# Seven products of block sums for eight products of blocks in the second shared network

## The chip, the cores and the metric

The kernel runs on one core of a Trainium2 chip. The metric is the device time in microseconds (us), as the median of several runs. A profiled execution gives the times of single instructions.

## The reference

128 samples `x` (64 x 256 each) go through three two-layer networks with a `relu` between the layers: one of five experts, chosen by the sample's type, and two shared ones. A gate (softmax over three values, made from row 0 of the three outputs) mixes them; then comes one step of a reaction and diffusion equation over the 64 x 256 plane of the sample.

```python
s0 = relu(x @ swi[0]) @ swo[0]          # swi: 2 x 256 x 1024, swo: 2 x 1024 x 256
s1 = relu(x @ swi[1]) @ swo[1]
eo = relu(x @ wi[type]) @ wo[type]
w = softmax(relu(concat(eo[:, 0], s0[:, 0], s1[:, 0]) @ g1) @ g2)
x = x + eo * w0 + s0 * w1 + s1 * w2
x = x + zX * lap_x(x) + zY * lap_y(x) + zR * x * (1 - x)
```

All is float32.

## The kernel before, in words

**Numbers.** A float32 operand is cut into a high part in the PE's fp32r format and a low part (the rest). A product is three matmuls: high x high, high x low, low x high. `XH`/`XL` are the two parts of a tile's columns, `SWH`/`SWL` those of the first weights, `HH`/`HL` those of the hidden values; `SWO` holds both parts of the second weights side by side, so one matmul of 512 columns and one of 256 make a block of a second product.

**Passes and steps.** The work is a list of passes, `PASSES`: two for the gate's rows, 22 expert units, and from `FIRST` on the shared networks. There are 16 tiles of 8 samples (512 columns in 4 blocks of 128), and a tile has two passes: an even one with the first shared network (b = 0) and an odd one with the second (b = 1). The last tile's odd pass is made in two halves of 256 columns (`HALVES`). A pass has 8 steps (`c`), one for each 128 of the 1024 hidden values; `g` counts steps over all passes. Each engine has a loop over `g`, which is the order of its work; nothing is planned at run time.

**PE.** In step `g` it makes the first product of `g` (`first_product`, line 946: for two blocks of 128 input rows, three matmuls each of 512 columns, lines 986 to 988, into one of three banks `hbank`) and then the second product of step `g - 2` (`second_product`, line 1028: four blocks, lines 1055 and 1056, summed over the pass in `acc[0..3]`).

**ACT and DVE.** ACT writes the high part of the hidden values of `g` (`hidden_high`, line 1160; `relu`, line 1166), DVE the low part (`hidden_low`, line 646; operation at line 658), which frees the bank and lets the second product run. At a pass's end, in step 1 of the next, ACT scales `acc` by the gate into `EO` (lines 1168 and 1185), and DVE adds the second half of `acc` (`evacuate`, lines 661 and 676), which frees `acc[j]`.

**Beside this.** In an odd pass DVE makes `residual` (line 689) in step 2, `add_shared` (line 697) for the first network in step 3, and `turn_tile` (line 600: the next tile's blocks, loaded by SP, are transposed into `XZ`) in step 4; ACT copies `XZ` to the high part (`tile_high_whole`, line 1158) and DVE subtracts for the low part (`tile_low_whole`, line 605) in step 5. In an even pass DVE makes `add_shared` for the second network of the tile before in step 1 and the equation in steps 2 to 6 (lines 703, 709, 713, 720, 726), with ACT's `quadratic` in step 2; SP moves halo rows of `Y` in between. The order of the parts in DVE's loop body matters here: in a step, `hidden_low(g)` comes before `evacuate`, and both before the block that begins `if FIRST <= n < NP - 1`.

**The end.** The last tile's results are made block by block, in the order 0, 2, 1, 3: `shared_sum` (line 737), `rows_last`, `react_last` (751), `add_x_last` (757), `add_row` (777), `result_last` (line 781; operation 786). POOL makes the sums of neighbours in `SS` (lines 1353 and 1354), SP stores blocks 1, 2 and 3 (line 1487).

Of the kernel before, what the change touches and what calls it, by code (L numbers as in the profile page):

```python
# [5 lines left out]
F32 = mybir.dt.float32  # L6
F32R = mybir.dt.float32r
I32 = mybir.dt.int32
ALU = mybir.AluOpType
# [75 lines left out]


def tile_of(n):
    kind, i = PASSES[n]
    return 0 if kind == PRE else 1 + i if kind == EXP else 1 + NU + i // 2
# [58 lines left out]
for _g, (_n, _c) in enumerate(CHUNKS):  # L148
    RING += [key for key in tile_parts(_n, _c) if key[0] > 1 and key[1] == 1] + [_g]
PLACE = {key: i for i, key in enumerate(RING)}  # L150


def next_tile(n, c):


    if c != (6 if n == FIRST - 1 else 4) or n < FIRST - 1 or n >= NP - 3:
# [85 lines left out]
def cond_resid_program(nc, x, itok, zx, zy, zr, wi, wo, swi, swo, g1, g2, out):  # L242
    eo_d = nc.dram_tensor("eo_scratch", (NS + NSLOT, S, D), F32, kind="Internal").ap()
    ctx = ExitStack()
    with ctx:
# [14 lines left out]
        XH = [sb(f"xh{i}", [128, 1024], F32R) for i in range(2)]  # L260
        XL = [sb(f"xl{i}", [128, 1024], F32R) for i in range(2)]
        RX = sb("rx", [128, 1024])
        XS = [sb(f"xs{i}", [128, 4, D]) for i in range(2)]
# [30 lines left out]
        with ExitStack() as early:  # L294
            EWH = [sb(f"ewh{i}", [128, 2, F], F32R, early) for i in range(2)]
            EWL = [sb(f"ewl{i}", [128, 2, F], F32R, early) for i in range(2)]
            EWO = [sb("ewo0", [128, NC, 2 * D], F32R, early)]

            with ExitStack() as first:
                RW0 = [sb(f"rw0{i}", [128, 1024], F32, first) for i in range(4)]  # L300
            EWO.append(sb("ewo1", [128, NC, 2 * D], F32R, early))
            RW = [sb(f"rw{i}", [128, 1024], F32, early) for i in range(4)]

# [9 lines left out]
        wx = sb("wx", [128, 6, NT])  # L313
        mask16 = sb("mask16", [128, NT])

        hbank = [ctx.enter_context(nc.psum_tensor(f"hbank{i}", [128, 512], F32)) for i in range(HRING)]
# [35 lines left out]
        lapy = sem("lapy")  # L352
        last_row = sem("last_row")
        itok_in = sem("itok_in")
        z_in = sem("z_in")
# [11 lines left out]

        XB, XZ = RW[0:2], RW[2]

        def unit_cols(a):  # L370
# [67 lines left out]
        def bank_free(key):  # L438

            i = RING[PLACE[key] - HRING]  # L440
            if isinstance(i, tuple):
                return t_free, T_AT[i]
            return (h_hi, i + 1 - 2 * NC) if upright(i) else low_done(i)
# [31 lines left out]
        def _(e):  # L475
# [117 lines left out]
            def turn_tile(t):  # L593

                if t == 0:
                    e.wait_ge(*cut_done(1 + NU, 2))
                else:
                    e.wait_ge(xt_lo, t)
                e.wait_ge(xb_in[t % 2], 256 * (t // 2 + 1))
                e.transpose(XZ[:], XB[t % 2][:]).then_inc(xz_done, 1)  # L600

            def tile_low_whole(t):
                tile = 1 + NU + t
                e.wait_ge(xt_hi, t + 1)
                e.tensor_tensor(XL[tile % 2][:], XZ[:], XH[tile % 2][:].bitcast(F32), ALU.subtract).then_inc(xt_lo, 1)

            def gate_masks():
# [52 lines left out]

            def evacuate(n):
# [6 lines left out]
                for j in block_order(n):  # L668
# [111 lines left out]

            def result_last(j):
                t = NT - 1
                rows = last_y[:, 3, :] if j == 2 else EO[1][:, j, :]
                e.wait_ge(dve_seq, AT["row", 2] if j == 2 else AT["rows", j])
                e.wait_ge(dve_seq, AT["last", 3] if j == 2 else AT["lapx", j])
                e.scalar_tensor_tensor(OT[t % 2][:, j, :], rows, WB[:, 4, t:t + 1], QQ[:, j, :], ALU.mult,
                                       ALU.add).then_inc(*V.up())
                AT["result", t, j] = V.n

            for g in range(G + LAG):  # L790
# [28 lines left out]
                if (n, c) == (2, 0):  # L819
                    evacuate(1)  # L820
                    cut_low(2, 2)
                if g < G and (n, c) != (1, NC - 1):
                    hidden_low(g)
# [9 lines left out]
                if g >= LAG and is_last(g - LAG) and CHUNKS[g - LAG][0] < NP - 2 and g - LAG != 2 * NC - 1:  # L833
                    evacuate(CHUNKS[g - LAG][0])
# [37 lines left out]
            add_x_last(2)  # L872
            rows_last(3)
            shared_sum(1)
            add_row(0)
# [3 lines left out]
            e.wait_ge(o_out[(NT - 1) % 2], 16 * ((NT - 1) // 2))  # L879
            result_last(1)  # L880
            shared_sum(3)
            result_last(2)
            react_last(3)
            add_x_last(3)
            result_last(3)

        @block.tensor
        def _(e):
# [138 lines left out]

            def second_product(g):
# [6 lines left out]
                e.wait_ge(*low_done(g))  # L1035
                if PASSES[n][0] == PRE:
# [7 lines left out]
                woc = weights(n)[2]  # L1044
                if c % 4 == 0:
                    e.wait_ge(*cut_done(weight_set(n), 2 + c // 4))
                order = list(block_order(n))
                for i, j in enumerate(order):
                    js = slice(i * 128, (i + 1) * 128)
                    if c == 0 and acc_before(n, j):  # L1050
# [3 lines left out]
                    else:  # L1054
                        e.matmul(acc[j][:, 0:2 * D], HH[:, g % NH, js], woc[:, c, :], start=(c == 0), stop=False)  # L1055
                        m = e.matmul(acc[j][:, D:2 * D], HL[:, g % NH, js], woc[:, c, 0:D], start=False, stop=last)  # L1056
                    if last:
# [20 lines left out]
            for g in range(G + LAG):  # L1078
# [33 lines left out]
                if (n, c) == (2, 0):  # L1112
                    second_product(g - 2)
                    second_product(g - 1)
                if g < G and (n, c) != (1, NC - 1):
                    first_product(g)
# [19 lines left out]
        def _(e):  # L1136
# [30 lines left out]

            def evacuate(n):
                kind, i = PASSES[n]
                for j in block_order(n):  # L1170
                    if kind == EXP:
# [60 lines left out]
            for g in range(G + LAG):  # L1232
# [14 lines left out]
                if (n, c) == (2, 0):  # L1247
                    cut_high(2, 2)
                if g < G and PASSES[n][0] != PRE:
                    hidden_high(g)  # L1250
                if 2 * NC <= g - LAG < G - 2 * NC and is_last(g - LAG):
                    evacuate(CHUNKS[g - LAG][0])
# [20 lines left out]
        def _(e):  # L1273
# [72 lines left out]
            e.tensor_tensor(FIRST_ROW[:, 0:128:16], ident[:, 0:128:16], ident[:, 0:128:16], ALU.add).then_inc(mats, 1)  # L1346

            t = NT - 1
            for j in LAST_ORDER:
                y = inner(t)[:, j, :]  # L1350
                e.wait_ge(dve_seq, AT["last", j])
                e.wait_ge(dve_seq, AT["result", t - 1])
                e.tensor_tensor(SS[:, j, 1:D - 1], y[:, 0:D - 2], y[:, 2:D], ALU.add).then_inc(lapx, 1)
                e.tensor_tensor(SS[:, j, 0:D:D - 1], y[:, 1:D:D - 3], y[:, 1:D:D - 3], ALU.add).then_inc(lapx, 1)

        @block.sync
        def _(e):
# [127 lines left out]
            for j in (1, 2, 3):  # L1485
                e.wait_ge(dve_seq, AT["result", t, j])
                e.dma_start(out_rows(out, t)[:, j * D:(j + 1) * D], OT[t % 2][:, j, :]).then_inc(o_out[t % 2], 16)
# [23 lines left out]
```

## Time and profile before

| | us |
|---|---|
| median of 3 runs (1135.97 to 1136.01) | 1135.98 |
| profiled execution | 1135.78 |
| its span, first to last instruction | 1134.3 |
| PE busy | 1128.2 (99%) |
| weight loads busy (PEld, beside PE) | 963.9 (85%) |
| DVE busy | 674.2 (59%) |
| ACT busy | 455.5 (40%) |
| POOL busy | 78.8 (7%) |

The span is what the profile covers; the profiled execution's own time is 1.5 us longer. "Busy" is time in which at least one instruction of the engine is shown running. Matmuls are pipelined: one is shown for longer than the distance to the next one's start, so the pace is read from starts.

### The profile page before, as it was taken

The page shows a single profiled execution, that of the slowest core. Times are in us where ns is not written, and L with a number is a line of the kernel's source. Part 1 is how long each engine was busy: PE and PEld are TensorE (multiplying, and loading weights), DVE is VectorE, ACT ScalarE, POOL GpSimd, SP SyncE. Part 2 cuts the span into 40 slices and gives each one's busy share as a digit, 9 for nine tenths or more (in the row PEclk, how much of TensorE's full clock was granted, in tenths as well). Part 3 has the DMA queues.
Part 4 walks back from the last instruction along what each step waited for, and adds up shares of the span by engine and source line. Part 5 has one row for each costly group of instructions (what it writes and reads, how often), then busy time and mean ns, then how long its engine had stood idle before and what let it go on. Part 6 is the DMA issues. An engine that isn't in the chain of part 4 may idle for free.

```text
span 1134.3 us, 16608 instructions
## 1 busy us (share of the span) xinstructions
PE 1128.2 (99%) x5968; PEld 963.9 (85%) x5968; DVE 674.2 (59%) x1007; ACT 455.5 (40%) x790; POOL 78.8 (7%) x123
## 2 busy tenths in 40 slices
PE   9999999999999999999999999999999999999998
PEld 8888888888888888888888888888888888888888
DVE  5655666666676645556546556555565465565556
ACT  3554655555565522333333323323333333233233
POOL 1211212112121000000000000000000000000001
PEclk9999999999999999999999999999999999999999
DMA  8655656566565413113123022031131230221200
GB/s 269 178 161 178 197 175 209 168 183 182 175 204 167 114 52 87 28 57 85 22 64 84 14 71 64 30 75 28 57 85 21 64 85 14 72 58 36 75 29 24
DMA packets 111251, 111.82 MB, mean 99 GB/s; under 512 B 78441, under 2 KB 87234, under 8 KB 111170
## 3 DMA queue, kind: packets, MB, share of 16 engines
q1 hardware_dynamic: 96738, 59.64, 19.4%
q0 software_dynamic: 13952, 50.60, 14.8%
q8 instruction: 47, 0.77, 0.3%
q10 hardware_dynamic: 480, 0.53, 0.2%
q14 instruction: 34, 0.28, 0.1%
HBM read 89.40 MB, written 17.04 MB: 94 GB/s over the span
## 4 chain that ended last, share of the span: by engine, by line
PE 99%; DVE 0%; issue 0%; POOL 0%; DVEq 0%; POOLq 0%
PE acc L1055 30%; PE hbank L986 16%; PE hbank L987 16%; PE acc L1056 15%; PE hbank L988 15%; PE acc L1024 1%; PE acc L1041 1%; PE acc L892 0%; PE tbank L934 0%; PE hbank L934 0%; PE acc L1025 0%; PE hbank L959 0%; PE hbank L1003 0%; PE hbank L1004 0%; PE hbank L1002 0%; PE hbank L960 0%
## 5 line engine op out<-in xcount | busy, mean ns | idle before, releaser
L658 DVE SCALAR_TENSOR_TENSOR hl<-hbank,hh 128x512 fp32r<-128x512 f32 (+1 forms) x416 | 272.0, 655 | 421.1 <-ACT hh L1166 420.8
L1166 ACT ACTIVATE hh<-hbank 128x512 fp32r<-128x512 f32 (+1 forms) x416 | 235.9, 568 | 564.7 <-PE hbank L988 561.3
L1055 PE MATMUL acc<-swo,hh 128*128 128x512 f32 x992 | 359.4, 396 | 0.0
L1056 PE MATMUL acc<-swo,hl 128*128 128x256 f32 x992 | 278.1, 280 | 0.0
L1055 PEld LDWEIGHTS acc<-swo,hh 128*128 128x128 f32 x992 | 186.4, 188 | 43.6
L986 PE MATMUL hbank<-xh,swh 128*128 128x512 f32 (+1 forms) x528 | 205.5, 389 | 0.0
L987 PE MATMUL hbank<-xl,swh 128*128 128x512 f32 (+1 forms) x528 | 205.1, 389 | 0.0
L988 PE MATMUL hbank<-xh,swl 128*128 128x512 f32 (+1 forms) x528 | 202.2, 383 | 0.0
L1056 PEld LDWEIGHTS acc<-swo,hl 128*128 128x128 f32 x992 | 187.4, 189 | 9.6
L1055 PE MATMUL acc<-ewo,hh 128*128 128x512 f32 x496 | 180.0, 395 | 0.0
L1056 PE MATMUL acc<-ewo,hl 128*128 128x256 f32 x496 | 139.1, 281 | 0.0
L986 PEld LDWEIGHTS hbank<-xh,swh 128*128 128x128 f32 x528 | 99.2, 188 | 23.2
L988 PEld LDWEIGHTS hbank<-xh,swl 128*128 128x128 f32 x528 | 99.6, 189 | 21.6
L1055 PEld LDWEIGHTS acc<-ewo,hh 128*128 128x128 f32 x496 | 93.1, 188 | 21.0
L987 PEld LDWEIGHTS hbank<-xl,swh 128*128 128x128 f32 x528 | 99.3, 188 | 10.1
L986 PE MATMUL hbank<-xh,ewh 128*128 128x512 f32 (+1 forms) x288 | 107.4, 373 | 0.0
L987 PE MATMUL hbank<-xl,ewh 128*128 128x512 f32 (+1 forms) x288 | 104.7, 364 | 0.0
L988 PE MATMUL hbank<-xh,ewl 128*128 128x512 f32 (+1 forms) x288 | 104.4, 363 | 0.0
L1056 PEld LDWEIGHTS acc<-ewo,hl 128*128 128x128 f32 x496 | 93.6, 189 | 4.2
L986 PEld LDWEIGHTS hbank<-xh,ewh 128*128 128x128 f32 x288 | 54.2, 188 | 9.9
L988 PEld LDWEIGHTS hbank<-xh,ewl 128*128 128x128 f32 x288 | 54.1, 188 | 9.5
L987 PEld LDWEIGHTS hbank<-xl,ewh 128*128 128x128 f32 x288 | 54.5, 189 | 4.5
(215 smaller groups left out, 973.5 us busy)
## 6 DMA issues: line engine op xcount, KB each, us to landing
rw<-in_L_cond_wi POOLq DMA_DIRECT2D x44, 512.0 KB, 4.4
rw<-in_L_cond_wo POOLq DMA_DIRECT2D x44, 512.0 KB, 4.8
eo_scratch<-eo SPq DMA_DIRECT2D x128, 64.0 KB, 2.4
xs<-in_x SPq DMA_DIRECT2D x16, 512.0 KB, 4.3
rw<-in_x SPq DMA_DIRECT2D x256, 32.0 KB, 2.3
ei<-eo_scratch SPq DMA_DIRECT2D x16, 512.0 KB, 5.5
xs<-in_x SPq DMA_DIRECT2D x126, 64.0 KB, 3.3
out<-ot SPq DMA_DIRECT2D x15, 512.0 KB, 6.3
```

What stands on the lines that cost most here:

```text
L658: e.scalar_tensor_tensor(h_slot(HL, g), bank[:, 0:w], 0.0, h_slot(HH, g).bitcast(F32), ALU.max, ALU.subtract).then_inc(h_lo, 1)
L986: e.matmul(to, wh[:, k, cs], xh[k], start=(k == 0), stop=False)
L987: e.matmul(to, wh[:, k, cs], xl[k], start=False, stop=False)
L988: i = e.matmul(to, wl[:, k, cs], xh[k], start=False, stop=(k == 1))
L1024: e.matmul(acc[0][:, 0:2 * D], HH[:, g % NH, hs], woc[:, f, :], start=(f == 0), stop=False)
L1041: e.matmul(acc[0][:, 0:D], HF[:, g % NH, :], raw_rows(n, 2 + c // 4)[:, c % 4, :], start=(c == 0), stop=last).then_inc(acc_done if last el ...
L1055: e.matmul(acc[j][:, 0:2 * D], HH[:, g % NH, js], woc[:, c, :], start=(c == 0), stop=False)
L1056: m = e.matmul(acc[j][:, D:2 * D], HL[:, g % NH, js], woc[:, c, 0:D], start=False, stop=last)
L1166: e.activation(h_slot(HU if upright(g) else HH, g), bank_of(g)[:, 0:w], ACT.Relu).then_inc(h_hi, 1)
```

## The change

**The products.** In the odd passes of tiles 1 to 14 (14 passes), the eight block products of a first product over two steps become seven. A step pair takes hidden values `p` and `p + 4` (of 8 groups of 128), two blocks of 128 input rows, and two halves of 256 columns: a 2 x 2 by 2 x 2 block product. It is made in the manner of Strassen and Winograd, from sums of the blocks. The sums of the weights (`SUMH`, `SUML`) are made once, by POOL, ACT and DVE; the sums of a tile's columns (`th`, `tl`) in the even pass ahead: four sums on DVE in step 0 (`column_sums`, in place in `XZ`), the high part on ACT in step 3, the low part on DVE in step 7. Each product is three matmuls of 256 columns.

**The corners.** Four of the products are added in one PSUM bank (corner), which between them must be copied out by ACT, since its running value is part of several results; DVE adds the other two banks (sides) to the copies. Then come `relu` and low part as before, but from three places: the top half of a pair (512 columns, in SBUF), the lower right (256, SBUF) and the lower left (256, PSUM).

**What moves.** The second products of a changed pass are cut in two around product D; the evacuation of the even pass is spread over steps 1 and 2 of the changed one; `add_shared` of the first network goes from step 3 to 7, `turn_tile` stays in step 4 (now behind the step's own work), ACT's copy of the tile goes to the end of step 5, and `tile_low_whole` from 5 to 6. SP gets two more loads (512 KB each) ahead of the loop over tiles.

**The end.** For block 3 of the last tile DVE makes the sum of neighbours and other steps itself (`last_block`), and POOL makes the result of block 2.

The diff, cut to its core:

```diff
+def seven(n):
+    kind, i = PASSES[n]
+    return kind == SH and i % 2 == 1 and i >= 3 and 0 <= n < NP - 2
...
@@ DVE @@
+            def column_sums(t):
+                x = [[half_block(XZ[:], k, h) for h in range(2)] for k in range(2)]
+                e.wait_ge(xt_lo, t + 1)
+                e.tensor_tensor(x[1][1], x[1][1], x[0][1], ALU.subtract).then_inc(*V.up())
+                e.wait_ge(dve_seq, V.n)
...
+            def column_sums_low(t):
+                e.wait_ge(ts_hi, t)
+                e.tensor_tensor(TL, XZ[:], TH.bitcast(F32), ALU.subtract).then_inc(ts_lo, 1)
...
+            def seven_step(g):
+                n, c = CHUNKS[g]
+                if c % 2 == 0:
+                    if c == 2:
+                        evacuate(n - 1, (3,))
+                    top_left_sum(g)
+                    if c >= 2:
+                        right_low(g - 1)
+                        left_low(g - 1)
+                    return
+                if c == 1:
+                    evacuate(n - 1, (0,))
+                top_right_sum(g)
+                if c == 1:
+                    evacuate(n - 1, (1,))
+                low_right_sum(g)
+                top_low(g - 1)
+                if c == 1:
+                    evacuate(n - 1, (2,))
...
-                    if b == 1 and c == 3:
+                    if b == 1 and c == (7 if seven(n) else 3):
                         add_shared(t, 0)
+                    if seven(n) and c == 4:
+                        turn_tile(t + 1)
+                    if seven(n) and c == 6:
+                        tile_low_whole(t + 1)
+                    if n == FIRST + 1 and c == 7:
+                        weight_sums_low()
+                    if b == 0 and seven(n + 1) and c == 0:
+                        column_sums(t)
+                    if b == 0 and seven(n + 1) and c == 7:
+                        column_sums_low(t)
...
+            scaled_rows()
...
-            result_last(1)
+            result_one()
             shared_sum(3)
-            result_last(2)
-            react_last(3)
-            add_x_last(3)
-            result_last(3)
+            last_block()
@@ PE @@
+            def seven_step(g):
...
+                def product(to, hi, lo, cols, start, stop):
+                    to = to.rearrange("p (j n) -> p j n", n=128)
+                    e.matmul(to, hi, cols[0], start=start, stop=False, skip_group_check=True)
+                    e.matmul(to, hi, cols[1], start=False, stop=False, skip_group_check=True)
+                    return e.matmul(to, lo, cols[0], start=False, stop=stop, skip_group_check=True)
...
+                if c % 2 == 0:
+                    prev = AT_CHUNK[n, 0]
+                    if c == 0:
+                        e.wait_ge(*low_done(prev - 3))
+                        e.wait_ge(ts_lo, SEVENS.index(n) + 1)
+                        e.wait_ge(dve_seq, AT["weight sums"])
...
+                    product(corner, wh[:, 0, at], wl[:, 0, at], x[0][0], True, False).then_inc(p_prod, 1)
...
+                    product(side, wh[:, 1, at], wl[:, 1, at], x[1][0], True, True).then_inc(p_prod, 1)
...
+                    of_sum(other, 3, y[0][1], True, False).then_inc(h_prod, 1)
+                    second_product(g - LAG, (0, 1))
+                    e.wait_ge(p_copy, 4 * q + 1)
+                    of_sum(corner, 0, y[0][0], False, False).then_inc(p_prod, 1)
+                    second_product(g - LAG, (2, 3))
+                    return
+                if c == 1:
+                    second_product(g - LAG, (0, 1))
+                e.wait_ge(p_copy, 4 * q + 2)
+                of_sum(other, 1, x[1][1], False, True).then_inc(p_prod, 1)
+                e.wait_ge(p_copy, 4 * q + 3)
+                of_sum(corner, 2, y[1][1], False, False).then_inc(p_prod, 1)
+                second_product(g - LAG, (2, 3) if c == 1 else None)
+                e.wait_ge(p_copy, 4 * q + 4)
+                product(corner, wh[:, 1, low], wl[:, 1, low], y[1][0], False, True).then_inc(h_prod, 1)
@@ ACT @@
+            def seven_step(g):
...
+                if c % 2 == 0:
+                    e.wait_ge(p_prod, 5 * q + 1)
...
+                    e.activation(TOP[q % 2][:, 0:256], corner, ACT.Copy).then_inc(p_copy, 1)
+                    if c == 2:
+                        evacuate(n - 1, (3,))
+                    if c >= 2:
+                        right_high(g - 1)
...
+                    e.activation(P5_ROOM, other, ACT.Copy).then_inc(p_copy, 1)
+                    if c >= 2:
+                        left_high(g - 1)
+                    e.wait_ge(p_prod, 5 * q + 3)
+                    e.activation(TOP[q % 2][:, 256:512], corner, ACT.Copy).then_inc(p_copy, 1)
+                    return
+                if c == 1:
+                    evacuate(n - 1, (0, 1))
+                e.wait_ge(p_prod, 5 * q + 5)
...
+                e.activation(LOW_RIGHT, corner, ACT.Copy).then_inc(p_copy, 1)
+                top_high(g - 1)
+                if c == 1:
+                    evacuate(n - 1, (2,))
+                if c == 5:
+                    tile_high_whole(PASSES[n][1] // 2 + 1)
...
+                if (n, c) == (FIRST + 1, 6):
+                    weight_sums_high()
+                if FIRST <= n < NP - 1 and seven(n + 1) and c == 3:
+                    column_sums_high(PASSES[n][1] // 2)
@@ SP @@
+            for p, a in enumerate((SS, QQ)):
+                e.dma_start(piece_view(a[:].rearrange("p j d -> p (j d)"), p),
+                            swi[1].rearrange("(k p) f -> p k f", p=128)[:, :, p * 512:(p + 1) * 512]).then_inc(raw_in, 16)
```

The products in PE's order are called A to G: A, D, F and G go to the corner bank, B to the one side, C and E to the other. A changed step pair has A, B, C and D in its even step and E, F and G in its odd one.

## Rows read from the trace of the kernel before

**Rows 1.** Page, parts 1, 2 and 5: PE's busy time, its clock, one weight load.

```profile
PE 1128.2 (99%) x5968; PEld 963.9 (85%) x5968; DVE 674.2 (59%) x1007; ACT 455.5 (40%) x790; POOL 78.8 (7%) x123
...
PEclk9999999999999999999999999999999999999999
...
L986 PEld LDWEIGHTS hbank<-xh,swh 128*128 128x128 f32 x528 | 99.2, 188 | 23.2
```

**Rows 2.** Waits of PE: who was waited for, us in total, times, longest.

```profile
PE acc L892 <- POOL ones L1276: 1.5, 1, 1.5
PE hbank L1076 <- DVE y L737: 0.4, 1, 0.4
```

**Rows 3.** Timeline, PE, even pass's start (679) and odd's (701): start, duration, instruction.

```profile
679.05 0.40 PE L986 MATMUL hbank<-xh,swh 128*128 128x512 f32 x1
...
701.34 0.40 PE L986 MATMUL hbank<-xh,swh 128*128 128x512 f32 x1
...
702.73 0.39 PE L1055 MATMUL acc<-swo,hh 128*128 128x512 f32 x1
...
704.13 0.40 PE L986 MATMUL hbank<-xh,swh 128*128 128x512 f32 x1
```

**Rows 4.** Timeline, PE, the halved pass: matmuls of 256 columns.

```profile
1107.96 0.35 PE L1066 MATMUL acc<-swo,hh 128*128 128x256 f32 x1
1108.14 0.28 PE L1067 MATMUL acc<-swo,hh 128*128 128x256 f32 x1
...
1108.38 0.28 PE L986 MATMUL hbank<-xh,swh 128*128 128x256 f32 x1
...
1109.82 0.28 PE L986 MATMUL hbank<-xh,swh 128*128 128x256 f32 x1
```

**Rows 5.** Timeline, DVE, the same even and odd pass.

```profile
684.66 1.65 DVE L676 SCALAR_TENSOR_TENSOR eo<-acc,wb,eo 128x256 f32<-128x256 f32 x4
686.35 1.23 DVE L697 TENSOR_TENSOR y<-y,eo 128x1024 f32<-128x1024 f32 x1
...
700.77 0.69 DVE L658 SCALAR_TENSOR_TENSOR hl<-hbank,hh 128x512 fp32r<-128x512 f32 x1 [0.90 <-ACT hh L1166]
...
713.66 1.24 DVE L600 STREAM_TRANSPOSE rw<-rw 128x1024 f32<-128x1024 f32 x1
716.51 0.69 DVE L658 SCALAR_TENSOR_TENSOR hl<-hbank,hh 128x512 fp32r<-128x512 f32 x1 [1.61 <-ACT hh L1166]
717.12 1.22 DVE L605 TENSOR_TENSOR xl<-rw,xh 128x1024 fp32r<-128x1024 f32 x1
```

**Rows 6.** Timeline, ACT, odd pass (512 and 1024 columns) and halved pass (256).

```profile
700.14 0.60 ACT L1166 ACTIVATE hh<-hbank 128x512 fp32r<-128x512 f32 x1 [2.19 <-PE hbank L988]
...
714.93 1.06 ACT L1158 ACTIVATE xh<-rw 128x1024 fp32r<-128x1024 f32 x1 [3.04 <-DVE rw L600]
...
1119.38 0.38 ACT L1166 ACTIVATE hh<-hbank 128x256 fp32r<-128x256 f32 x1 [1.06 <-PE hbank L988]
```

**Rows 7.** Timeline, DVE, the end of the kernel.

```profile
1128.98 0.47 DVE L737 SCALAR_TENSOR_TENSOR y<-acc,wb,y 128x256 f32<-128x256 f32 x1
...
1130.35 0.41 DVE L751 TENSOR_TENSOR qq<-qq,y 128x256 f32<-128x256 f32 x1
...
1131.45 0.48 DVE L786 SCALAR_TENSOR_TENSOR ot<-eo,wb,qq 128x256 f32<-128x256 f32 x1
```

**Rows 8.** Timeline, PE, the end of the kernel.

```profile
1129.51 0.70 PE L1076 MATMUL hbank<-y,g1s 128*128 128x256 f32 x2 [0.37 <-DVE y L737]
```

**Rows 9.** Timeline, DVE, around the start of tile 1's even pass.

```profile
455.55 0.69 DVE L658 SCALAR_TENSOR_TENSOR hl<-hbank,hh 128x512 fp32r<-128x512 f32 x1 [2.10 <-ACT hh L1166]
458.33 0.69 DVE L658 SCALAR_TENSOR_TENSOR hl<-hbank,hh 128x512 fp32r<-128x512 f32 x1 [2.10 <-ACT hh L1166]
458.94 0.28 DVE L766 TENSOR_REDUCE sm<-g1s 128x1 f32<-128x128 f32 x1
...
459.45 0.21 DVE L770 TENSOR_SCALAR sm<-sm,wb 128x1 f32<-128x1 f32 x1
```

More of the change, by code:

```diff
@@ L84, in blocks, with pair_at, hidden_chunk @@
     return width(n) // 128
+def seven(n):
+    kind, i = PASSES[n]
+    return kind == SH and i % 2 == 1 and i >= 3 and 0 <= n < NP - 2
+SEVENS = [n for n in range(NP) if seven(n)]
+def pair_at(g):
+    n, c = CHUNKS[g]
+    return 4 * SEVENS.index(n) + c // 2
+def hidden_chunk(n, c):
+    return c // 2 + 4 * (c % 2) if seven(n) else c
 def tile_of(n):
@@ L148 @@
 for _g, (_n, _c) in enumerate(CHUNKS):
-    RING += [key for key in tile_parts(_n, _c) if key[0] > 1 and key[1] == 1] + [_g]
+    if not seven(_n):
+        RING += [key for key in tile_parts(_n, _c) if key[0] > 1 and key[1] == 1] + [_g]
 PLACE = {key: i for i, key in enumerate(RING)}
 def next_tile(n, c):
+    if seven(n):
+        return None
     if c != (6 if n == FIRST - 1 else 4) or n < FIRST - 1 or n >= NP - 3:
@@ L301, in cond_resid_program @@
             EWO.append(sb("ewo1", [128, NC, 2 * D], F32R, early))
-            RW = [sb(f"rw{i}", [128, 1024], F32, early) for i in range(4)]
+            RW = [sb(f"rw{i}", [128, 1024], F32, early) for i in range(3)]
+            with ExitStack() as sums_room:
+                th = sb("th", [128, 1024], F32R, sums_room)
+            RW.append(sb("rw3", [128, 1024], F32, early))
         EI = [sb(f"ei{i}", [128, 4, D]) for i in range(2)]
@@ L353, in cond_resid_program @@
         last_row = sem("last_row")
+        last_two = sem("last_two")
+        p_prod = sem("p_prod")
+        p_copy = sem("p_copy")
+        p_sum = sem("p_sum")
+        p_hi = sem("p_hi")
+        p_lo = sem("p_lo")
+        raw_in = sem("raw_in")
+        w_sum = sem("w_sum")
+        sum_hi = sem("sum_hi")
+        ts_hi = sem("ts_hi")
+        ts_lo = sem("ts_lo")
         itok_in = sem("itok_in")
@@ L440, in bank_free @@
             i = RING[PLACE[key] - HRING]
+            if not isinstance(key, tuple) and seven(CHUNKS[key][0] - 1) and CHUNKS[key][1] < 3:
+                return p_sum, 3 * pair_at(AT_CHUNK[CHUNKS[key][0] - 1, 7]) + 2
             if isinstance(i, tuple):
@@ new lines, in column_sums_low, with weight_sums_low @@
+            def column_sums_low(t):
+                e.wait_ge(ts_hi, t)
+                e.tensor_tensor(TL, XZ[:], TH.bitcast(F32), ALU.subtract).then_inc(ts_lo, 1)
+            def weight_sums_low():
+                for i, a in enumerate((SS, QQ)):
+                    e.wait_ge(sum_hi, i + 1)
+                    e.tensor_tensor(SUML[:, 2 * i:2 * i + 2, :], a[:].rearrange("p j d -> p (j d)").rearrange(
+                        "p (k f) -> p k f", k=2), SUMH[:, 2 * i:2 * i + 2, :].bitcast(F32), ALU.subtract).then_inc(*V.up())
+                AT["weight sums"] = V.n
@@ L821, in _ @@
                     cut_low(2, 2)
-                if g < G and (n, c) != (1, NC - 1):
+                if g < G and c == 0 and seven(n - 1):
+                    right_low(g - 1)
+                    left_low(g - 1)
+                if g < G and seven(n):
+                    seven_step(g)
+                elif g < G and (n, c) != (1, NC - 1):
                     hidden_low(g)
@@ L832, in _ @@
                         cut_low(ws, p)
-                if g >= LAG and is_last(g - LAG) and CHUNKS[g - LAG][0] < NP - 2 and g - LAG != 2 * NC - 1:
+                if (g >= LAG and is_last(g - LAG) and CHUNKS[g - LAG][0] < NP - 2 and g - LAG != 2 * NC - 1 and
+                        not (g < G and seven(n))):
                     evacuate(CHUNKS[g - LAG][0])
@@ L1044, in second_product @@
                 woc = weights(n)[2]
-                if c % 4 == 0:
+                if c % 4 == 0 and not seven(n):
                     e.wait_ge(*cut_done(weight_set(n), 2 + c // 4))
-                order = list(block_order(n))
+                order, f = list(block_order(n)), hidden_chunk(n, c)
                 for i, j in enumerate(order):
-                    js = slice(i * 128, (i + 1) * 128)
+                    if js is not None and j not in js:
+                        continue
+                    at = slice(i * 128, (i + 1) * 128)
                     if c == 0 and acc_before(n, j):
@@ L1114, in _ @@
                     second_product(g - 1)
+                if g < G and seven(n):
+                    seven_step(g)
+                    continue
                 if g < G and (n, c) != (1, NC - 1):
@@ L1248, in _ @@
                     cut_high(2, 2)
[L1249 removed]
+                if g < G and c == 0 and seven(n - 1):
+                    right_high(g - 1)
+                    left_high(g - 1)
+                if g < G and seven(n):
+                    seven_step(g)
+                elif g < G and PASSES[n][0] != PRE:
                     hidden_high(g)
[L1251 removed]
+                if 2 * NC <= g - LAG < G - 2 * NC and is_last(g - LAG) and not seven(n):
                     evacuate(CHUNKS[g - LAG][0])
```

182 lines of the change are left out of this document (166 added, 16 removed).

## The prediction

> **What bounds the kernel now.** I read the page's first part, then the waits of PE, then PE's timeline in two even passes and in the last passes, and last the DVE and ACT timelines in the same stretches. The page gives PE busy for 1128.2 of 1134.3 us, at a granted clock of full speed (2.4 GHz) in all 40 slices [rows 1]. Busy PE is not proof of a bound, but the waits are: PE waited for another engine twice, 1.5 us at the start and 0.4 us at the end [rows 2]. So between them PE streams without a break, and only two things can move the time: how long the stream of matmuls takes, and any new wait in it. DVE and ACT have idle time, and matter only as the ones PE could come to wait for.
>
> The pace of the stream: six matmuls of 512 columns take 702.73 - 701.34 = 1.39 us, and four (512, 256) pairs of a second product take 704.13 - 702.73 = 1.40 us, together one step of 2.79 us [rows 3]. Where all matmuls have 256 columns, twelve take 1109.82 - 1108.38 = 1.44 us, 0.120 us each [rows 4]. A short matmul thus costs 0.120, not 1.39 / 12 = 0.116: halving the columns costs 4% of the time.
>
> **Term 1, seven products for eight.** Two steps of a changed pass had 12 first matmuls of 512 columns, 2.78 us. They now have 7 products of 3 matmuls of 256 columns: 21 x 0.120 = 2.52 us. Gain 0.26 us per pair, four pairs in each of 14 passes: 56 x 0.26 = 14.6 us off. The rows are printed to 0.01 us, so 0.26 has some 0.02 either way: 13.4 to 15.7. The second products stay as they are, only cut in two halves.
>
> The Trainium skill (TensorE: Matmul & The Clock Gate, Back-to-back issue gap) gives an isolated gap of N / 2.4 + 2.5 ns. By it the pair would save 12 x 215.8 - 21 x 109.2 = 296 ns, an estimate of 16.6 us in all. The 0.120 and 0.232 us of the rows are both above its 0.109 and 0.216, and the measurement decides.
>
> **Term 2, a new wait at the head of every changed pass.** PE may not issue the first product of the pass before `ts_lo` has been raised, and that is raised by `column_sums_low`, one DVE subtraction of 128x1024. It stands behind `hidden_low` of step 7 of the even pass, which in its turn waits for the first product of that very step. In the row, that `hidden_low` starts at 700.77, while PE starts the next pass at 701.34 [rows 3, 5]. DVE issues the next instruction 0.61 us behind the start of an L658 (716.51 to 717.12), so `column_sums_low` would start at 701.38, and the operation of the same shape and types, L605, takes 1.22 us [rows 5]: done at 702.60. From the end of a DVE result to PE's start is 1128.98 + 0.47 = 1129.45 to 1129.51, 0.06 us [rows 7, 8]. So PE starts at 702.66 and not at 701.34: 1.32 us. An interrupted stream also restarts slower: at 1107.96 the matmul takes 0.18 us until the next one instead of 0.12 [rows 4]; I add 0.06. That gives 1.38 us, 14 times: 19.3 us on. Nothing hides it: the work that needs no column sum (the products A and B, and the second products of the even pass's steps 6 and 7) is queued behind the waiting instruction, and PE is in order. Bounds: 1.30 (no restart cost) to 1.50 (the wait also exposes the first weight load of 0.19), 18.2 to 21.0.
>
> **Term 3, waits inside a changed pass.** With A to G for the seven products in PE's order, a pair takes 7 x 0.36 + 2 x 1.40 = 5.32 us: A 0, B 0.36, C 0.72, half a second product 1.08, D 1.78, the other half 2.14, E 2.84, F 3.20, a whole second product 3.56, G 4.96. A matmul is shown 0.28 us, so a product ends 0.16 us after the next starts; ACT follows within 0.03 us. A 256-wide ACT operation takes 0.38 us and a 512-wide one 0.60 [rows 6]; on DVE 0.41 to 0.47 [rows 7] and 0.69 [rows 5]. The copy of A is done at 0.93 and D wants it at 1.78; the copy of C, behind the right-half `relu`, at 1.69 against 2.84; the copy of D at 2.71 against 3.20; the copy of F at 4.13 against 4.96. On DVE the top half is finished some 0.15 us into the next pair, and the second product that reads it comes at 1.08; the left half at 2.5 against 3.56. So ACT does 6 x 0.38 + 0.60 = 2.9 us and DVE 2.8 us in 5.32: no wait. What else lies in the pass fits too: `turn_tile` (1.24), `tile_low_whole` (1.22) [rows 5] and `residual` (1024 columns too) now stand behind `left_low` and shift `top_right_sum` to 4.2 or 4.5, and with it the last relu, by less than the 1 us there is; ACT's `tile_high_whole` (1.06 [rows 6]) ends 0.46 us into the next pair, before A's copy is due at 0.55. The tightest is the first pair, where F comes at 3.90 and ends at 4.42 behind the moved evacuations of blocks 0 and 1 on ACT (done 4.2): F's copy ends at 4.83 and G wants it at 4.96, and its weight load about 0.1 us earlier. I take 0.05 us a pass, 0.7 us; bounds 0 and 0.3 us a pass (one ACT operation late), 4.2.
>
> **Term 4, the even passes.** `column_sums` adds four dependent DVE operations of 128x512 in step 0. No row has that shape; 0.41 us at 256 [rows 7] and 1.22 at 1024 [rows 5] bound it, and 0.68 on the line between them, with 0.04 between dependent ones, makes 2.9 us in all. Counted from PE's start of the pass, `add_shared` (now at step 7, 1.2 us) and the last pair's two halves are off DVE at 2.05, `hidden_low` of step 0 at 2.82 (its product 1.39 + 0.16, ACT 0.03 + 0.60, then 0.03 and 0.61), the sums at 5.7, `hidden_low` of step 1 at 6.2. The evacuation of four blocks (1.65 us for four, so 0.39 apart, with 0.48 for one) then ends its blocks at 6.7, 7.1, 7.5 and 7.9, and PE starts on them at 6.97, 7.32, 7.67 and 8.02 of its stream. Just in time: 0; up to 0.15 us a pass, 2.1. `add_shared` behind it moves from 686.35 - 679.05 = 7.3 to 8.1, which delays SP's halo copies and `lap_y` by 0.8 us; DVE has that much idle time in each of steps 3 to 7.
>
> In the first even pass of a changed tile there is no such cover. `weight_sums_low` puts two operations of 1.22 us in front: `hidden_low` of step 7 starts at 455.55 [rows 9], the two end at 458.5, where the next `hidden_low` starts today at 458.33, then `last_factors` (458.94 to 459.66, 0.7) and the sums run until 462.6, `hidden_low` of step 1 until 463.2, and block 3 is evacuated at 464.9 while PE, which starts the pass 0.57 us after that `hidden_low` of step 7, wants it at 456.1 + 8.02 = 464.1. 0.9 us on, once; bounds 0 and 2. The loads of the raw weights (two issues on SP), POOL's four sums and ACT's two copies lie in the 15 us before, all off PE's path.
>
> **Term 5, the end.** Today the last shared sum starts at 1128.98 and the last result at 1131.45 for 0.48 [rows 7]. Then come five DVE operations instead of the four in between (the result of block 2 has gone to POOL, which holds it up by no more than one operation): 0.42, 0.4, 0.48, 0.41, 0.41 with two or three dependent gaps end near 1131.7. 0.2 us off; bounds 0.5 off, 0.3 on (DVE slowed by POOL beside it). SP issues block 2 before 3, and has it earlier.
>
> Sum: 1135.78 (the profiled execution; its span is 1134.3 and 1.5 lies around it) - 14.6 + 19.3 + 0.7 + 0.9 - 0.2 = 1141.9. The median of the runs, 1135.98, is 0.2 above the profiled one, so **1142.1**.
>
> **Rivals.** (a) *The wait is short and the change pays.* Place: PE's wait for `ts_lo`. It decides at 14.6 / 14 = 1.04 us. For it: DVE might be freed earlier than L658's spacing says, or take the SBUF operation faster. Against it: 1.22 us is the duration in all rows of L605, and the wait cannot be under 0.04 + 1.22 + 0.06 us unless `hidden_low` comes sooner. At no wait at all it would be 1122; at half, 1132. Chance 0.09, mostly for an error in my reading of the order. (b) *The two cancel within 0.2%* (1133.7 to 1138.3, about what a measurement of this kernel can tell from no change): gain at 15.7, wait at 1.25, everything else nothing: 1137.5. Chance 0.09. (c) *Copies come late inside the pairs*: four handovers a pair with slacks of 0.5 to 1.1 us, and if DVE or ACT takes 0.25 us longer than its rows at the tightest of them in most pairs, 56 x 0.15 to 56 x 0.25 come on top: 1150 to 1156. Against it: the engines are half idle in the pair. Chance 0.08. (d) *Short matmuls run at the pace of the weight loads*, each shown with 188 ns [rows 1]: 21 x 0.19 = 3.99 us a pair instead of 2.78, 68 us on, 1224 in all. Against it stand twelve matmuls in 1.44 us, with the same order of operands [rows 4]. Chance 0.01.
>
> The skill's same section has measured spacings in real kernels of 81 ns for 128 columns and 131 ns for 512; on the line between them 256 columns would cost 98 ns, and 21 of those against 12 of 131 would lose 0.49 us a pair, an estimate of 27 us slower before any wait. It is rival (d) in kind; the 232 and 120 ns of this trace speak against it.
>
> The likeliest case, the forecast with 0.73, spans 1138.3 to 1148. Faster 0.09 is (a), same 0.09 is (b), slower 0.82 the rest. The range 1138.0 to 1148.0 leaves out (a), most of (b), (c) and (d).
>
> **What the profile after would show.** Term 1: 21 matmuls of 256 columns, spaced by 0.120 us, in a pair of 5.32 us. Term 2: PE's waits led by a DVE subtraction into `tl`, 14 times, near 1.3 us each; PE's busy time falls by about 15 us while the span grows. Terms 3 and 4: waits for ACT's copies or for evacuations small or missing. The prediction is wrong if PE starts the changed pass without a gap, if the gap is under 1.04 us, or if waits inside the pairs sum to more than 5 us.

## The result, and the profile after

| | us |
|---|---|
| before, median of 6 | 1135.97 |
| after, median of 6 (1140.22 to 1140.91) | 1140.49 |
| ratio after / before | 1.0042, 95% interval 1.0031 to 1.0053 |
| span before, after | 1134.3, 1138.6 |

The change makes the kernel 4.5 us slower, inside the predicted range and on the forecast side. Its products do save time, some 16 us; a single wait at the head of each changed pass takes 20. Each time below is a median; it leaves out one run of e6 that took 1363.08 us at a mean granted clock of 0.753.

The first part of the page after, against [rows 1]: PE is busy for 13 us less in a span that is 4.3 us longer, with 504 more matmuls, and DVE and ACT have 110 and 102 us more work.

```profile
PE 1115.2 (98%) x6472; PEld 975.4 (86%) x6472; DVE 784.0 (69%) x1305; ACT 557.3 (49%) x1086; POOL 86.1 (8%) x127
```

PE's waits after (us in total, times, longest), the answer to [rows 2]:

```profile
PE hbank L1230 <- issue: 16.8, 14, 1.2
PE acc L1080 <- POOL ones L1600: 1.5, 1, 1.5
PE acc L1303 <- DVE hl L811: 0.4, 1, 0.4
PE hbank L1324 <- DVE y L890: 0.4, 1, 0.4
```

One new line matters: 14 waits of 1.2 us, as many as there are changed passes (the other new one, 0.4 us on L1303, stands at 27.8 us, long before the shared networks). L1230 is the first of the three matmuls of a product. The profile doesn't name who was waited for ("issue"), so the timelines of the two engines have to be laid side by side. PE at the head of the first changed pass, and of the one answering to [rows 3]:

```profile
478.23 0.28 PE L1304 MATMUL acc<-swo,hl 128*128 128x256 f32 x1
479.70 0.35 PE L1230 MATMUL hbank<-xh,swh 128*128 128x256 f32 x1 [1.19 <-issue]
479.89 0.28 PE L1231 MATMUL hbank<-xl,swh 128*128 128x256 f32 x1
480.01 0.28 PE L1232 MATMUL hbank<-xh,swl 128*128 128x256 f32 x1
...
680.57 0.39 PE L1174 MATMUL hbank<-xh,swh 128*128 128x512 f32 x1
...
704.17 0.36 PE L1230 MATMUL hbank<-xh,swh 128*128 128x256 f32 x1 [1.20 <-issue]
704.37 0.28 PE L1231 MATMUL hbank<-xl,swh 128*128 128x256 f32 x1
...
725.45 0.39 PE L1174 MATMUL hbank<-xh,swh 128*128 128x512 f32 x1
```

DVE at the same place as the first of these (against [rows 5]):

```profile
477.77 0.69 DVE L811 SCALAR_TENSOR_TENSOR hl<-hbank,hh 128x512 fp32r<-128x512 f32 x1 [0.90 <-ACT hh L1417]
478.38 1.22 DVE L692 TENSOR_TENSOR tl<-rw,th 128x1024 fp32r<-128x1024 f32 x1
480.75 0.43 DVE L725 TENSOR_TENSOR first_part<-hbank,first_part 128x256 f32<-128x256 f32 x1 [1.16 <-ACT first_part L1457]
```

L692 is `column_sums_low`. It starts 0.61 us behind `hidden_low` of step 7 and ends at 479.60; PE starts at 479.70. The last matmul before the gap, at 478.23, is a short one, normally followed after 0.12 us; here the next comes after 1.47 (1.48 in the other 13 passes), and the one behind that after 0.19 or 0.20. The gap thus costs 1.36 + 0.08 = 1.44 us. The passes tell the same: an even pass with the gap takes 704.17 - 680.57 = 23.60 us against 22.29 before [rows 3], a changed pass 725.45 - 704.17 = 21.28. Together +1.31 - 1.01 = +0.30, and 14 x 0.30 = 4.2 of the 4.3 us.

### The profile page after: what moved, and what is told of

It is laid out like the page before. It is cut to its first block, busy times and chain, and to the rows that moved or that the text cites. A ratio compares the mean times of both kernels' runs of the same rounds, so it can differ in the third digit from the quotient of the medians.

```text
span 1138.6 us, 18531 instructions
## 1 busy us (share of the span) xinstructions
PE 1115.2 (98%) x6472; PEld 975.4 (86%) x6472; DVE 784.0 (69%) x1305; ACT 557.3 (49%) x1086; POOL 86.1 (8%) x127
## 4 chain that ended last, share of the span: by engine, by line
PE 97%; issue 2%; DVE 1%; DMA 1%; ACT 0%; POOLq 0%; POOL 0%; DVEq 0%
PE acc L1303 30%; PE acc L1304 15%; PE hbank L1175 11%; PE hbank L1176 11%; PE hbank L1174 11%; PE hbank L1230 3%; PE hbank L1231 3%; PE hbank L1232 3%; PE tbank L1231 1%; PE tbank L1230 1%; PE tbank L1232 1%; PE acc L1212 1%; DMA rw<-in_L_cond_wo 1%; PE acc L1080 0%; PE acc L1287 0%
## 5 line engine op out<-in xcount | busy, mean ns | idle before, releaser
L1303 PE MATMUL acc<-swo,hh 128*128 128x512 f32 x992 | 359.9, 394 | 0.0
L1417 ACT ACTIVATE hh<-hbank 128x512 fp32r<-128x512 f32 (+1 forms) x304 | 169.5, 560 | 362.0 <-PE hbank L1176 358.8
L811 DVE SCALAR_TENSOR_TENSOR hl<-hbank,hh 128x512 fp32r<-128x512 f32 (+1 forms) x304 | 194.4, 641 | 218.6 <-ACT hh L1417 218.5
L1303 PEld LDWEIGHTS acc<-swo,hh 128*128 128x128 f32 x992 | 186.2, 188 | 35.6
L1303 PE MATMUL acc<-ewo,hh 128*128 128x512 f32 x496 | 180.1, 395 | 0.4 <-DVE hl L811 0.4
L1176 PE MATMUL hbank<-xh,swl 128*128 128x512 f32 (+1 forms) x304 | 116.8, 384 | 0.0
L1175 PE MATMUL hbank<-xl,swh 128*128 128x512 f32 (+1 forms) x304 | 116.4, 383 | 0.0
L1174 PE MATMUL hbank<-xh,swh 128*128 128x512 f32 (+1 forms) x304 | 115.5, 380 | 0.0
L1303 PEld LDWEIGHTS acc<-ewo,hh 128*128 128x128 f32 x496 | 93.1, 188 | 21.9 <-DVE hl L811 0.8
L829 DVE SCALAR_TENSOR_TENSOR eo<-acc,wb,eo 128x256 f32<-128x256 f32 x124 | 55.0, 477 | 37.0 <-ACT eo L1500 35.2
L1174 PEld LDWEIGHTS hbank<-xh,swh 128*128 128x128 f32 x304 | 57.2, 188 | 11.5
L1176 PEld LDWEIGHTS hbank<-xh,swl 128*128 128x128 f32 x304 | 57.1, 188 | 11.0
L1175 PEld LDWEIGHTS hbank<-xl,swh 128*128 128x128 f32 x304 | 57.3, 188 | 6.3
```

The lines of the kernel that those rows point to most:

```text
L811: e.scalar_tensor_tensor(h_slot(HL, g), bank[:, 0:w], 0.0, h_slot(HH, g).bitcast(F32), ALU.max, ALU.subtract).then_inc(h_lo, 1)
L1174: e.matmul(to, wh[:, k, cs], xh[k], start=(k == 0), stop=False)
L1175: e.matmul(to, wh[:, k, cs], xl[k], start=False, stop=False)
L1176: i = e.matmul(to, wl[:, k, cs], xh[k], start=False, stop=(k == 1))
L1303: e.matmul(acc[j][:, 0:2 * D], HH[:, g % NH, at], woc[:, f, :], start=(c == 0), stop=False)
L1417: e.activation(h_slot(HU if upright(g) else HH, g), bank_of(g)[:, 0:w], ACT.Relu).then_inc(h_hi, 1)
```

## The experiments

Two accounts of the gap stood against each other: PE waits there for the one subtraction that stands behind `hidden_low`; or the hand-over to the new form of the pass (low parts, banks, operands) makes it. The kernel before was timed anew beside each group of runs: 1135.91 us beside e1, e2, e3 and e5, 1136.38 beside e4, e6 and e7. The ratios below are to these, and a difference between runs of the two groups is good to some 0.5 us.

**e1: the subtraction one step earlier.**

```diff
-                    if b == 0 and seven(n + 1) and c == 7:
+                    if b == 0 and seven(n + 1) and c == 6:
                         column_sums_low(t)
```

> The changed kernel with the subtraction that raises ts_lo one step earlier in DVE's order (step 6 of the even pass, ahead of result, not behind hidden_low of step 7). Theory (PE waits at the head of each changed pass for that one subtraction, which is queued behind hidden_low): in the changed kernel's trace PE's start is late by 1.48 - 0.12 = 1.36 us and the next matmul by 0.08, 14 times, so 20 us go: 1140.5 - 20.2 = 1120.3, and no PE idle time at these places. Rival (the gap comes from the hand-over between the passes itself: low parts of steps 5 to 7, other banks, other operands): the gap stays, 1138 to 1141.

Measured: 1120.14 us, ratio to the kernel before 0.9861 (0.9844 to 0.9877). The waits of PE in this kernel:

```profile
PE acc L1080 <- POOL ones L1600: 1.5, 1, 1.5
PE hbank L1324 <- DVE y L890: 0.4, 1, 0.4
```

and PE around one changed pass:

```profile
695.64 0.28 PE L1304 MATMUL acc<-swo,hl 128*128 128x256 f32 x1
695.76 0.28 PE L1230 MATMUL hbank<-xh,swh 128*128 128x256 f32 x1
...
716.97 0.39 PE L1174 MATMUL hbank<-xh,swh 128*128 128x512 f32 x1
```

The gap is gone, 0.12 us from matmul to matmul across the hand-over. So the place of one DVE instruction among the others was worth 20.3 us, and the sign of the result hung on it. The hand-over itself costs nothing, and nor does the wait for the weight sums, which stands at the head of the pass here too. On DVE, the subtraction now lies in front of `result` in step 6, and `hidden_low` of step 7 follows it at once:

```profile
693.02 1.22 DVE L692 TENSOR_TENSOR tl<-rw,th 128x1024 fp32r<-128x1024 f32 x1
694.15 1.28 DVE L879 SCALAR_TENSOR_TENSOR ot<-ss,wb,qq 128x1024 f32<-128x1024 f32 x1
695.35 0.69 DVE L811 SCALAR_TENSOR_TENSOR hl<-hbank,hh 128x512 fp32r<-128x512 f32 x1
```

**e2: PE's wait two products later.**

```diff
                     if c == 0:
                         e.wait_ge(*low_done(prev - 3))
-                        e.wait_ge(ts_lo, SEVENS.index(n) + 1)
-                        e.wait_ge(dve_seq, AT["weight sums"])
...
                     if c == 0:
                         e.wait_ge(*low_done(prev - 1))
+                        e.wait_ge(ts_lo, SEVENS.index(n) + 1)
+                        e.wait_ge(dve_seq, AT["weight sums"])
```

> The changed kernel with PE's waits for ts_lo and for the weight sums moved from ahead of product A to ahead of product C, the first that reads the column sums. Theory: DVE finishes the subtraction at the same moment, and A and B (0.72 us) are made meanwhile, so each gap shrinks from 1.36 to 0.64 us: 14 x 0.72 = 10.1 us off, 1130.4. Rival (hand-over between the passes): a wait moved behind two products changes nothing, 1140.5.

Measured: 1130.77 us, ratio 0.9956 (0.9940 to 0.9973), 9.7 us below the changed kernel where 10.1 were expected. A and B run, and the rest of the wait stands in front of C:

```profile
700.11 0.28 PE L1232 MATMUL hbank<-xh,swl 128*128 128x256 f32 x1
700.87 0.35 PE L1230 MATMUL hbank<-th,sumh 128*128 128x256 f32 x1 [0.49 <-issue]
```

0.76 - 0.12 = 0.64 us are left of the gap. The wait moved with the wait instruction, which the hand-over account excludes.

**e3: the subtraction twice.**

```diff
             def column_sums_low(t):
                 e.wait_ge(ts_hi, t)
+                e.tensor_tensor(TL, XZ[:], TH.bitcast(F32), ALU.subtract).then_inc(*V.up())
+                e.wait_ge(dve_seq, V.n)
                 e.tensor_tensor(TL, XZ[:], TH.bitcast(F32), ALU.subtract).then_inc(ts_lo, 1)
```

> The changed kernel with the subtraction into tl made twice, one after the other, before ts_lo is raised. Theory: 1.22 + 0.04 us more on the path, 14 times: 17.6 us on, 1158.1. Rival (the gap is not set by this subtraction): DVE has idle time there (1.16 us before the next one), so 0 to 3 us on.

Measured: 1179.22 us, 38.7 above the changed kernel and not 17.6. The direction is the theory's, the size is not. Even passes take 24.86 us, 1.26 longer than in the changed kernel, just the added operation. But the changed passes take 22.83 instead of 21.28. The windows of one of them (PE, PEld, DVE, ACT, POOL busy, then the granted clock, DMA share, GB/s) show why:

```profile
910.54:912.00 1.46, 1.46 (x10) 1.45 (x11) 0.40 (x1) 0.49 (x2) 0.00 (x0) 0.89 0.84 118
912.00:914.00 2.00, 2.00 (x8) 1.73 (x7) 0.02 (x1) 0.46 (x2) 0.00 (x0) 0.50 0.78 229
914.00:916.00 2.00, 2.00 (x11) 1.82 (x10) 0.00 (x0) 0.62 (x3) 0.00 (x0) 0.73 0.88 330
916.00:918.00 2.00, 2.00 (x17) 1.86 (x16) 1.91 (x5) 1.78 (x5) 0.00 (x0) 1.00 0.44 170
```

PE had stood still from the matmul at 907.80 to that at 910.54. It then ran at full clock for 1.1 us, at half (0.50, 1.2 GHz) until about 915, and at full clock again. A pair of matmuls of 512 and 256 columns took 0.62 us in this stretch:

```profile
911.68 0.61 PE L1305 MATMUL acc<-swo,hh 128*128 128x512 f32 x1
912.09 0.41 PE L1306 MATMUL acc<-swo,hl 128*128 128x256 f32 x1
912.30 0.63 PE L1305 MATMUL acc<-swo,hh 128*128 128x512 f32 x1
```

This costs 1.55 us a pass, in all 14: 14 x (1.26 + 1.55) = 39.3 us. The longer gap is paid again after it has ended. The fall doesn't come at a fixed distance from the restart: in windows of 0.5 us it lies 0.3 us behind it in the first of the 14 passes, 1.1 in the one shown and 1.5 in the last. The Trainium skill (TensorE: Matmul & The Clock Gate, What's actually happening) names two states of this gate, half and full; the 0.50 of the window fits that.

**e7: half of the subtraction more.**

```diff
             def column_sums_low(t):
                 e.wait_ge(ts_hi, t)
+                e.tensor_tensor(TL[:, 0:512], XZ[:, 0:512], TH[:, 0:512].bitcast(F32), ALU.subtract).then_inc(*V.up())
+                e.wait_ge(dve_seq, V.n)
                 e.tensor_tensor(TL, XZ[:], TH.bitcast(F32), ALU.subtract).then_inc(ts_lo, 1)
```

> The changed kernel with half of the subtraction (512 of 1024 columns, about 0.70 us with its wait) made once more before it: between the changed kernel (gap 1.36 us, granted clock full) and e3 (gap 2.6 us, after which the clock was 0.5 for some 3 us and the pass 1.55 us longer). If the clock stays up at a gap of 2.1 us: 14 x 0.70 = 9.8 us on, 1150.3. If it falls as in e3: 1150.3 + 14 x 1.55 = 1172.

Measured: 1165.87 us, between the two. From one matmul to the next it is now 2.20 us at every head (1.48 in the changed kernel, 2.74 in e3):

```profile
945.26 0.28 PE L1306 MATMUL acc<-swo,hl 128*128 128x256 f32 x1
947.47 0.36 PE L1232 MATMUL hbank<-xh,swh 128*128 128x256 f32 x1 [1.92 <-issue]
```

Of the 14 passes behind them, nine take 22.8 us and five 21.3. The windows of two neighbours:

```profile
947.47:970.30 22.83, 22.83 (x148) 21.15 (x149) 14.56 (x30) 12.95 (x32) 0.00 (x0) 0.93 0.28 74
994.63:1015.92 21.29, 21.29 (x149) 19.83 (x149) 14.56 (x30) 12.96 (x32) 0.00 (x0) 1.00 0.25 80
```

Both have the same number of matmuls on PE; the mean clock differs. Expected from this: 14 x 0.73 + 9 x 1.54 = 24.1 us on; measured 25.4. The rest is lost ahead of the first changed pass, which starts 2.41 us later than in the changed kernel, where the added operation accounts for 0.73. The trace has a wait of PE of 1.1 us at 22.6 us that the changed kernel's doesn't have; what makes it isn't shown.

**e5: the price of short matmuls alone.** In the kernel before, the first products of the same 14 passes are made in halves:

```diff
+                if PASSES[n][0] == SH and PASSES[n][1] % 2 == 1 and PASSES[n][1] >= 3 and n < NP - 2:
+                    for h in range(2):
+                        part = to[:, 2 * h:2 * h + 2, :]
+                        for k in range(2):
+                            a, b = xh[k][:, 2 * h:2 * h + 2, :], xl[k][:, 2 * h:2 * h + 2, :]
+                            e.matmul(part, wh[:, k, cs], a, start=(k == 0), stop=False)
+                            e.matmul(part, wh[:, k, cs], b, start=False, stop=False)
+                            i = e.matmul(part, wl[:, k, cs], a, start=False, stop=(k == 1))
+                    i.then_inc(h_prod, 1)
+                    return
```

> The kernel before, with each first product of 512 columns in the odd passes of tiles 1 to 14 cut into two of 256 columns: the same columns in 24 matmuls a pair instead of 12, no seven products. It measures the price of short matmuls alone. Theory from the changed kernel's trace (0.1185 us a short one, 0.2317 a long one): 24 x 0.1185 - 2.78 = 0.064 us a pair, 56 pairs, 3.6 us on, 1139.6. By the prediction's 0.120: 0.10 a pair, 5.6 on, 1141.6. Rival (a short matmul costs just half): 1136.0. Rival (d) of the prediction (the 0.19 us of the weight load sets the pace): 100 us on.

Measured: 1143.26 us, ratio 1.0067 (1.0050 to 1.0084), 7.4 us on where I had expected 3.6, and 5.6 by the prediction's pace. From the changed kernel's trace I had read 0.1185 us for a short matmul; where twelve follow each other it is the 0.120 of the prediction:

```profile
704.03 0.28 PE L988 MATMUL hbank<-xh,swh 128*128 128x256 f32 x1
704.39 0.28 PE L988 MATMUL hbank<-xh,swh 128*128 128x256 f32 x1
...
706.88 0.28 PE L988 MATMUL hbank<-xh,swh 128*128 128x256 f32 x1
...
709.74 0.28 PE L988 MATMUL hbank<-xh,swh 128*128 128x256 f32 x1
```

A pair of steps takes 709.74 - 704.03 = 5.71 us instead of 5.58: 0.10 by the 24 short matmuls, and 0.03 in the second products beside them, which nothing here explains. The 0.13 times 56 is 7.3 of the 7.4. In e1 a pair is 21.21 / 4 = 5.30 us. So against eight products in equally short matmuls, the seven save 0.41 us a pair, and 0.13 of it is given back because they can't be long. Rival (d), by which the 0.19 us of a weight load would set the pace, is excluded (it would have cost 100 us).

**e6: how much slack the copies have.** On top of e1, in every pair:

```diff
+                e.activation(LOW_RIGHT, corner, ACT.Copy).then_inc(spare, 1)
+                e.wait_ge(spare, q + 1)
                 e.activation(LOW_RIGHT, corner, ACT.Copy).then_inc(p_copy, 1)
```

> e1 with ACT's copy of the corner after product F made twice in every pair (once into the same place, then again; 0.41 us later for everything behind it). It tests the slacks of the prediction's term 3. Theory: G waits only in the first pair of a pass, where the slack is used up already (G's matmul at 709.17 takes 0.16 us to the next one instead of 0.12); the other three pairs have 0.7 us. 14 x 0.41 = 5.7 us on, 1125.8. Rival (c) (the copies are tight in every pair): 56 x 0.4 = 23 us on, 1143. Rival (slack everywhere): 1120.1.

Measured: 1126.31 us, ratio 0.9911 (0.9891 to 0.9931), 6.2 us above e1. The changed passes take 21.63 instead of 21.21 us, and PE waits once in each:

```profile
PE hbank L1231 <- ACT later_part L1479: 2.8, 14, 0.2
```

The wait is in the first pair, whose evacuations stand ahead of the copy; the other three pairs take a delay of 0.41 us without a trace of it. 14 x 0.42 are 5.9 us; the first changed pass starts 0.5 us later than in e1, behind a wait of PE of 0.5 us at 21.6 us, and that is the rest. The run delays the copy after F and what follows it on ACT; how late the copies after A, C and D could come by themselves it doesn't test. Rival (c), tight handovers in every pair, would have cost 23 us.

**e4: the old end of the kernel,** on top of e1. `scaled_rows`, `result_one` and `last_block` are gone, POOL again makes all of block 3's neighbour sums, and:

```diff
-            result_one()
+            result_last(1)
             shared_sum(3)
-            last_block()
+            result_last(2)
+            react_last(3)
+            add_x_last(3)
+            result_last(3)
...
-            e.tensor_tensor(OT[t % 2][:, 2, :], EO[0][:, 3, :], QQ[:, 2, :], ALU.add).then_inc(last_two, 1)
```

> e1 (subtraction early) with the end of the kernel as it was before the change: block 3's results by the old steps, block 2's result on DVE. In the changed kernel's trace the last shared sum starts at 1133.17 and the last result ends at 1136.30, 3.13 us, with one DVE operation of 1.04 us beside POOL's 0.73 us one; in the kernel before it is 2.95 us. Theory (POOL beside DVE takes the saving back): 2.95 us again and 1119.9, a difference that only the trace can show. Rival (the prediction's term 5, 0.2 us saved by the new end): 3.3 us or more, 1120.4.

Measured: 1120.13 us, ratio 0.9856 (0.9840 to 0.9873); its time can't be told from e1's. The traces can be. The changed kernel, DVE at the end, to be read against [rows 7]:

```profile
1133.17 0.48 DVE L890 SCALAR_TENSOR_TENSOR y<-acc,wb,y 128x256 f32<-128x256 f32 x1
1133.68 0.42 DVE L951 TENSOR_TENSOR ss<-y 128x254 f32<-128x254 f32 x1
1134.02 0.34 DVE L952 TENSOR_SCALAR eo<-y,wb 128x256 f32<-128x256 f32 x1
1134.47 1.04 DVE L956 SCALAR_TENSOR_TENSOR ss<-ss,wb,eo 128x256 f32<-128x256 f32 x1
1135.43 0.41 DVE L959 TENSOR_TENSOR qq<-qq,y 128x256 f32<-128x256 f32 x1
1135.88 0.42 DVE L961 TENSOR_TENSOR ot<-ss,qq 128x256 f32<-128x256 f32 x1
```

POOL, in the same stretch:

```profile
1134.50 0.73 POOL L1696 TENSOR_TENSOR ot<-eo,qq 128x256 f32<-128x256 f32 x1 [0.34 <-DVE eo L952]
```

and e4, DVE:

```profile
1113.25 0.48 DVE L890 SCALAR_TENSOR_TENSOR y<-acc,wb,y 128x256 f32<-128x256 f32 x1
...
1115.73 0.48 DVE L939 SCALAR_TENSOR_TENSOR ot<-eo,wb,qq 128x256 f32<-128x256 f32 x1
```

From the last shared sum to the last result: 3.13 us with the new end, 2.96 with the old. The operation on the new path that runs beside POOL's takes 1.04 us where its kind takes 0.48, and these 0.56 us are more than the reordering saves. The old path has such an operation too, block 2's result: 0.87 us at 1113.84, beside POOL's sum of neighbours. The Trainium skill (SBUF — State Buffer, Who interferes with whom) has this as a port pair for which DVE and POOL compete when a DVE operation has two inputs in SBUF; this row has two, and agrees.

## Why the prediction was right, and where its terms were off

It forecast 1142.1 and a slower kernel, with the wait at the head of the pass as the cause. It is slower, and by that wait. The differences between the traces of before, after, e1 and e4 give each term:

| term | predicted | measured |
|---|---|---|
| 1 and 3: products, and waits inside the pass | -14.6 + 0.7 | -15.8 |
| 2: the wait at the head, 14 times | +19.3 | +20.0 |
| 4: first even pass, weight sums | +0.9 | 0 |
| 5: the end | -0.2 | +0.2 |

For the profiled execution the forecast was 1141.9, and 1140.22 came. The 1.7 us between them are misses of 1.9 and 0.9 us downwards and 0.7 and 0.4 upwards: the wait was understood, but the last microsecond of the agreement is partly luck.

**Terms 1 and 3.** Without the gap (e1) an even and a changed pass take 22.24 + 21.21 = 43.45 us, against 22.29 + 22.30 = 44.59 before: 1.14 us saved a tile, 14 x 1.14 = 16.0, the rows being good to some 0.1; the spans give 15.8. I had 1.04 gross and 0.99 net, so the 15.8 lies at the edge of my bounds. The term that was mis-sized is the pace of 0.120 in a changed pair: the short matmuls came at 0.118 to 0.119, and with 84 of them that is some 0.1 us a pass. My figure came from twelve in a row, and in the pair they lie in shorter groups between the long ones; that this makes the difference isn't shown. It explains the changed pass, which is 22.30 - 21.21 = 1.09 us shorter. The other 0.05 us are in the even pass, 22.24 instead of 22.29, though its matmuls are the same as before; nothing here explains them. The wait before G in the first pair was there, 0.04 us (0.16 us to the next matmul instead of 0.12); in e6, where the copy comes 0.41 us later, this is the one place that has no slack for it.

**Term 2.** Each number of the step held: 0.61 us behind `hidden_low` (477.77 to 478.38), 1.22 for the operation, and then 0.10 instead of 0.06 to PE's start. Against e1 the gap costs 23.60 + 21.28 - 43.45 = 1.43 us a tile. e1, e2 and e3 show that it is this instruction: earlier, waited for later, or made longer, the time follows. The kernel without the wait was put at 1122; e1 measured 1120.14, lower by the misses in the other terms.

**Term 4** had a wrong shape: `column_sums` works on half of the columns of one block of input rows, 256 wide and not 512. In the trace its four operations take 1.8 us and not 2.9:

```profile
503.81 0.41 DVE L681 TENSOR_TENSOR rw<-rw 128x256 f32<-128x256 f32 x1
504.26 0.43 DVE L683 TENSOR_TENSOR rw<-rw 128x256 f32<-128x256 f32 x1
...
505.98 0.69 DVE L811 SCALAR_TENSOR_TENSOR hl<-hbank,hh 128x512 fp32r<-128x512 f32 x1 [0.37 <-ACT hh L1417]
```

So in the later even passes DVE was idle again before `hidden_low` of step 1, and in the first one the evacuation of the four blocks ended at 463.55, before the 464.1 at which I had PE want the last: PE doesn't wait there. The 0.9 us never existed.

**Term 5** had the right bound (0.3 on, DVE slowed by POOL) and the wrong value. I had put the cost of POOL at "no more than one operation" for block 2, and left out of the sum that it is block 3's operation that is held up. The trace of before had a row that shows the size of it: block 2's result on DVE takes 0.87 us beside POOL's sum of neighbours, where the same line takes 0.48 alone.

```profile
1129.56 0.87 DVE L786 SCALAR_TENSOR_TENSOR ot<-y,wb,qq 128x256 f32<-128x256 f32 x1
...
1129.53 0.61 POOL L1353 TENSOR_TENSOR ss<-y 128x254 f32<-128x254 f32 x1 [2.16 <-DVE y L737]
```

So the 2.95 us of the old end held a slowed operation already, and my five operations at 0.4 to 0.48 us held none.

**The rivals.** (a), that the wait would be short, and (b), that both would cancel, fall with the gap of 1.36 us, above the 1.04 from which (a) decides. But e1 shows how near the other side was: one line apart. (c) falls with the list of PE's waits in the changed kernel, where none is for a copy, and with e6; (d) falls with e5.

## What to carry to other kernels

When a change makes the bounding engine wait for a new operand, find the operation that raises its semaphore and what is queued ahead of it on its own engine: 1.22 us of work on an engine that is a third idle cost more than a saving of one product in eight, and moving it by one step gave 20 us back. If an operand can't be ready, wait at its first reader and not at the head of the group; that alone gave back half. And read a saving in matmuls at the pace of the new, shorter shape: 0.13 of 0.41 us a pair went to the shortness.

## What the runs showed of the hardware

The cost of a gap in PE's stream jumps in these kernels between 1.5 and 2.7 us, counted from matmul to matmul. After 1.48 us the granted clock stayed full, 14 times of 14; after 2.20 us it fell to half in nine of 14 passes, after 2.74 us in all 14, and each fall cost another 1.55 us. It came 0.3 to 1.5 us after PE had started again, and half speed lasted over 3 us each time, so most of the price is paid when the wait has long ended. Nothing in the trace of before hinted at this, and my expectation for e3 was wrong by more than half because of it.
